# Where channel attention's two norms stand: inside the stages around them instead of between them

## The reference, cut to what matters

```python
f = jax.nn.gelu(h @ W1[l] + b1[l], approximate=False)
h = layer_norm(h + f @ W2[l] + b2[l], ln2_s[l], ln2_b[l])        # l = 3: the last of four layers
...
h = h + _L0_attn_ref(_layernorm(h, axis=-1), W_qkv, W_proj, b_proj, temp)   # channel attention
h = h + _L0_ffn_ref(_layernorm(h, axis=-1), Wg, bg, W1, b1, W2, b2)         # gates, then experts
...
def _L0_attn_ref(x, W_qkv, W_proj, b_proj, temp):      # per batch row, 8 heads of 24 channels
    q = q / jnp.linalg.norm(q, axis=1, keepdims=True)
    k = k / jnp.linalg.norm(k, axis=1, keepdims=True)
    attn = jax.nn.softmax(jnp.einsum('bnhd,bnhe->bhde', q, k) * temp, axis=-1)
    y = jnp.einsum('bhde,bnhe->bnhd', attn, v).reshape(b, n, c)
    return y @ W_proj + b_proj
```

## Time and profile before

| what | us |
|---|---|
| median of 3 runs (lowest, highest) | 1809.26 (1800.43, 1809.82) |
| the profiled execution, device time | 1813.13 |
| its span | 1811.3 |
| PE, DVE, ACT, POOL busy in the span | 1465.9, 1236.5, 980.9, 815.2 |
| PE's last product of layer 3 ends | 1003.27 |
| first products of channel attention start | 1037.99 |
| last product of channel attention ends | 1138.40 |
| the gates are complete (DVE reads them) | 1171.25 |

### The profile page before, as it was taken

The page is one execution under the profiler, slowest core; times in us unless marked ns, Lnnn a source line. Parts: engine busy times, 40 slices in busy tenths (PEclk is TensorE's granted clock), DMA queues, the critical chain, the costliest instruction groups (busy, mean ns, idle before and its releaser), DMA issues.

```text
span 1811.3 us, 39511 instructions
## 1 busy us (share of the span) xinstructions
PE 1465.9 (81%) x13098; PEld 1256.1 (69%) x13098; DVE 1236.5 (68%) x3514; ACT 980.9 (54%) x2393; POOL 815.2 (45%) x1175
## 2 busy tenths in 40 slices
PE   2789799997998888988989488669478887499991
PEld 2578677786777777877778377269457666499991
DVE  6878876889768896688976722434478886444444
ACT  1578635887348883378843133245258872055550
POOL 7786235773347733378523200145365511145540
PEclk9799999999999999999999678579789996599996
DMA  4644004470026530174800000167345501267765
GB/s 114 163 89 106 1 1 123 105 145 11 1 62 146 115 60 1 25 182 89 226 2 1 14 1 1 47 207 244 115 97 119 102 2 47 102 198 243 239 199 182
DMA packets 144278, 177.87 MB, mean 98 GB/s; under 512 B 22096, under 2 KB 106128, under 8 KB 143952
## 3 DMA queue, kind: packets, MB, share of 16 engines
q1 hardware_dynamic: 136784, 158.18, 34.0%
q0 software_dynamic: 7296, 17.18, 2.8%
HBM read 132.96 MB, written 42.34 MB: 97 GB/s over the span
## 4 chain that ended last, share of the span: by engine, by line
PE 53%; DVE 23%; issue 8%; POOL 8%; DMA 4%; ACT 3%; SPq 1%; POOLq 0%; DVEq 0%; ACTq 0%
PE bank L1498 7%; PE bank L663 7%; DVE ptl L821 4%; PE bank L575 4%; DVE neg_max L814 3%; PE bank L427 3%; PE bank L445 2%; PE bank L1484 2%; PE bank L447 2%; PE bank L446 2%; PE bank L449 2%; PE bank L448 2%; DVE xx L788 2%; PE bank L540 2%; DVE row_b L821 1%
## 5 line engine op out<-in xcount | busy, mean ns | idle before, releaser
L703 ACT ACTIVATE prob<-bank,neg_max 128x192 f32<-128x192 f32 (+1 forms) x960 | 412.6, 440 | 117.5 <-DVE neg_max L814 108.9
L814 DVE TENSOR_REDUCE neg_max<-bank 128x2 f32<-128x384 f32 (+1 forms) x480 | 272.2, 569 | 70.6 <-PE bank L540 69.9
L575 PE MATMUL bank<-ident,prob 128*128 128x128 f32 x1536 | 272.1, 290 | 48.3 <-DVE ptl L821 36.1
L716 ACT ACTIVATE pth<-bank 128x384 f16<-128x384 f32 (+1 forms) x480 | 245.9, 512 | 5.7 <-PE bank L575 5.6
L821 DVE TENSOR_TENSOR ptl<-bank,pth 128x384 f16<-128x384 f32 (+1 forms) x352 | 204.5, 581 | 10.5 <-ACT pth L716 10.0
L575 PEld LDWEIGHTS bank<-ident,prob 128*128 128x128 f32 x1536 | 161.7, 142 | 65.0 <-DVE ptl L821 47.6
L670 ACT ACTIVATE xx<-bank 128x256 fp32r<-128x256 f32 x256 | 96.3, 390 | 176.1 <-PE bank L427 172.6
L540 PE MATMUL bank<-kx,qx 96*128 96x192 bf16 (+1 forms) x960 | 166.8, 255 | 1.4 <-DVE xx L788 1.1
L754 ACT ACTIVATE fbuf<-bank,b 128x512 f32<-128x512 f32 x96 | 66.0, 687 | 165.0 <-PE bank L449 165.0
L596 PE MATMUL bank<-v,pth 128*128 128x33 bf16 x1152 | 137.8, 179 | 21.5 <-DVE ptl L821 18.5
L663 PE MATMUL bank<-w,fbuf 128*128 128x192 f32 x768 | 140.7, 326 | 1.9 <-DVE h L914 1.9
(11 more groups left out here) (304 smaller groups left out, 4644.7 us busy)
## 6 DMA issues: line engine op xcount, KB each, us to landing
xn<-in_e_seg SPq DMA_DIRECT2D x34, 768.0 KB, 6.7
w<-in_e_w SPq DMA_DIRECT2D x23, 576.0 KB, 4.3
qk_rows<-fbuf SPq DMA_DIRECT2D x128, 96.0 KB, 2.3
qx<-qk_rows SPq DMA_DIRECT2D x35, 288.0 KB, 4.1
kx<-qk_rows SPq DMA_DIRECT2D x35, 288.0 KB, 5.9
qk_rows<-w SPq DMA_DIRECT2D x80, 96.0 KB, 2.3
qx<-qk_rows SPq DMA_DIRECT2D x35, 192.0 KB, 4.7
kx<-qk_rows SPq DMA_DIRECT2D x35, 192.0 KB, 5.4
```

Source lines behind the costliest of these rows:

```text
L575: last = nc.tensor.transpose(bank[BT[p % 2]][:, c * P:c * P + P], probs_at(p, banded, c * P, P), ident[:, :])
L703: nc.scalar.activation(probs_at(p, banded, qt * n, n), scores_at(p, n)[:, qt, :], ACT.Exp, bias=neg_max[:, b % 2, hd, qt:qt + 1], scale=1. ...
L716: nc.scalar.activation(high_at(p, banded), bank[BT[p % 2]][:, 0:n], ACT.Copy).then_inc(hi_ready.sem, 1)
L814: nc.vector.tensor_reduce(neg_max[:, b % 2, hd, :], scores_at(p, D if banded else S), AX.X, ALU.max, negate=True).then_inc(max_ready.sem, 1)
```

## The change

The norm in front of channel attention and its turns leave their own stage:

- `dve_tail`, `pool_tail`, layer 3 alone: the statistics and the root of this norm for a group follow the affine of that group's second norm; its `dve_normalise` follows one iteration later, ahead of the next group's affine. The order of results on the shared counter is the new table `NORMED_LAST`.
- `under` hangs the turn of group 0 into step 16 of the feed-forward and that of group 1 into step 24. DVE splits group 0 (`channels(0)`) at the head of its iteration 3 and group 1 at the head of iteration 4.
- The turns of groups 2 and 3 and the `dve_normalise` of group 3 stand in the first two iterations of the batch loop. Batch b now waits for its own tiles (`xx_ready`) and for the release of the last feed-forward banks (`y_read`).
- The norm behind channel attention goes into the batch loop: DVE does the statistics of a group after iterations 2, 4, 6 and 8, its `dve_normalise` after iterations 3, 5 and 7 and after the loop. POOL does the roots between its powers.
- SP issues the ten loads of constants for this stage after layer 3's attention instead of after layer 3. Two memsets on POOL move ahead of the tail. PE waits for the lists and the last residual sum in front of the first gate product instead of implicitly through the norm.

No instruction of computation is added or removed.

```diff
@@ under
+            if channels:
+                steps[2 * FC + 4] = lambda: channels(0)
+                steps[NG * FC] = lambda: channels(1)
@@ dve_tail
+            def channels(g):
+                for t in range(GT * g, GT * g + GT):
+                    dve_split(dve, L, t, t)
...
+                if g >= NG - 1 and not opening:
+                    channels(g - NG + 1)
                 if g:
                     dve_residual(dve, ch, it, 1, g - 1)
                     dve_stats(dve, ch, it, 1, g - 1, y_read)
+                if g >= 2 and not opening:
+                    dve_normalise(dve, ch, it, norm_at(it, 0, g - 2), g - 2)
...
                 if g + 2 < NG:
                     out(g + 2)
+                if g and not opening:
+                    dve.wait_ge(h_ready.sem, h_ready.at(it, normed(2, GT * g - 1)))
+                    dve_stats(dve, ch, it, 0, g - 1, None)
@@ pool_tail
+                if g and not opening:
+                    scale(0, g - 1)
@@ sync
-            sp.wait_ge(h_ready.sem, h_ready.at(L, 0))
+            sp.wait_ge(sums_ready.sem, sums_ready.at(L - 1, NT))
@@ gpsimd
-            for g in range(NG):
-                pool_rstd(pool, ch, L, g + 1, g, 1e-5)
             for b in range(B):
...
+                if b and b % 2 == 0:
+                    pool_rstd(pool, ch, L, NG + b // 2, b // 2 - 1, 1e-5)
@@ scalar
-            for t in range(NT):
-                act_split(act, L, t, t)
             for b in range(B + 1):
                 if b < B:
                     act_xc_front(act, b)
+                if b < 2:
+                    xc_split(2 + b)
@@ vector
-            dve_norm_in(dve, ch, L, 0, 0)
...
                 if b:
                     dve_xc_out(dve, b - 1)
-            dve.wait_ge(xc_o_ready.sem, xc_o_ready.at(0, NT))
-            dve_norm_in(dve, ch, L, 1, None)
+                if b == 0:
+                    for t in range(2 * GT, 3 * GT):
+                        dve_split(dve, L, t, t)
+                    dve_normalise(dve, ch, L - 1, norm_at(L - 1, 0, 3), 3)
+                    for t in range(3 * GT, 4 * GT):
+                        dve_split(dve, L, t, t)
+                if b >= 3 and b % 2:
+                    dve_normalise(dve, ch, L, NG + (b - 3) // 2 + 1, (b - 3) // 2)
+                if b and b % 2 == 0:
+                    dve.wait_ge(xc_o_ready.sem, xc_o_ready.at(0, 2 * b))
+                    dve_stats(dve, ch, L, 0, b // 2 - 1, None)
+            dve_normalise(dve, ch, L, 2 * NG, NG - 1)
@@ tensor
-            for t in range(NT):
-                pe_transpose(pe, L, t, t, xn, xn_ready, 0, t + 1)
             pe.wait_ge(wa_ready.sem, wa_ready.at(L, 1))
-            pe.wait_ge(xx_ready.sem, xx_ready.at(L, NT))
...
+            pe.wait_ge(y_read.sem, y_read.at(L - 1, NT))
             for b in range(B + 1):
                 if b < B:
+                    pe.wait_ge(xx_ready.sem, xx_ready.at(L, 2 * b + 2))
                     pe_xc_front(pe, b)
                     pe_xc_gram(pe, b)
+                if b == 1:
+                    xc_turn(3)
+                    pe.wait_ge(xx_ready.sem, xx_ready.at(L, NT))
...
+                if b == 0:
+                    xc_turn(2)
```

More of the change, by code:

```diff
@@ L366, in normed, with norm_at @@
             return GT * NORMED.index((k, t // GT)) + t % GT + 1
+        def norm_at(it, k, g):
+            return (NORMED_LAST if it == LAYERS - 1 else NORMED).index((k, g)) + 1
         def turn_at(t, inside):
@@ L512, in early_steps, with under @@
             return list(zip(at, OPENING))
-        def under(turn, out=None, first=None):
+        def under(turn, out=None, first=None, channels=None):
             steps = {}
@@ L939, in dve_normalise @@
                 last.then_inc(xn_ready.sem, 1)
-        def dve_norm_in(dve, ch, it, half, turn):
-            for g in range(NG + 2):
-                if g < NG:
-                    dve_stats(dve, ch, it, half, g, None)
-                if 1 <= g <= NG:
-                    dve_normalise(dve, ch, it, half * NG + g, g - 1)
-                if turn is not None and g >= 2:
-                    for t in range(GT * (g - 2), GT * (g - 1)):
-                        dve_split(dve, it, turn * NT + t, t)
         def dve_affine(dve, ch, it, n, g, w):
@@ L970, in dve_tail @@
         def dve_tail(dve, ch, it, opening):
-            first = lambda g: NORMED.index((1, g)) + 1
-            second = lambda g: NORMED.index((2, g)) + 1
+            first = lambda g: norm_at(it, 1, g)
+            second = lambda g: norm_at(it, 2, g)
+            def channels(g):
+                for t in range(GT * g, GT * g + GT):
+                    dve_split(dve, L, t, t)
             def out(g):
@@ L1819, in pool_layer @@
                     pool_scale(pool, it, f)
+                if not opening:
+                    nc.gpsimd.memset(xc_nh[:, :], -0.5)
+                    nc.gpsimd.memset(xc_one[:, :], 1.0).then_inc(zeroed.sem, 1)
+                    pool.wait_ge(zeroed.sem, 2)
                 pool_tail(pool, ch, it, opening)
@@ L1841, in _ @@
                 .then_inc(lists_ok.sem, 1)
-            for g in range(NG):
-                pool_rstd(pool, ch, L, NG + g + 1, g, 1e-5)
+            pool_rstd(pool, ch, L, 2 * NG, NG - 1, 1e-5)
             pool_seq(pool, 0)
@@ L1888, in first_split, with xc_split @@
                 return lambda t, inside=False: act_split(act, it, t, t, inside)
+            def xc_split(g):
+                for t in range(GT * g, GT * g + GT):
+                    act_split(act, L, t, t)
             def act_layer(it, opening):
@@ L2105, in first_open, with xc_turn @@
                 pe_open(pe, it, kind, i, wa, first_turn(it), lambda n: (it, n))
+            def xc_turn(g):
+                for t in range(GT * g, GT * g + GT):
+                    pe_transpose(pe, L, t, t, xn, xn_ready, 0, t + 1)
             def pe_layer(it, opening):
@@ L2112, in pe_layer @@
                                 lambda g: pe_out_group(pe, it, wb, g),
-                                (lambda kind, i: first_open(it + 1, kind, i)) if opening else None))
+                                (lambda kind, i: first_open(it + 1, kind, i)) if opening else None,
+                                None if opening else xc_turn))
             for kind, i in OPENING:
@@ L2149, in _ @@
                                                    third[0:4, t * P:t * P + P], ident[0:4, 0:4])
+                if g == 1:
+                    pe.wait_ge(lists_in.sem, 32)
+                    pe.wait_ge(xc_o_ready.sem, xc_o_ready.at(0, 2 * B))
                 if 1 <= g <= NG:
```

8 lines of the change are left out of this document (3 added, 5 removed).

## The result

The changed kernel takes 1790.62 us (median of 7 runs, 1785.42 to 1793.25), the kernel before 1808.28 (7 runs, 1800.43 to 1814.6): a ratio of 0.9896, 95% interval 0.9869 to 0.9924, which is 14 to 24 us. The forecast was 1795.9 us, that is 13.4 us less, with a range of 1787.0 to 1806.0. The profiled executions stand further apart than the medians: 1785.42 against 1813.13, 27.7 us.

The account below looks back on a forecast made before the run. TensorE was taken to bound the tail, with two norm stretches where it waits for VectorE. Gains of 9.8 and 5.4 less 1.75 made 13.4 us off 1809.26, so 1795.9 us, range 1787 to 1806.

Parts of the forecast that it names:

- Part 1: Tail, step 16: TensorE stalls some 6 us for VectorE's splits of group 0's turn and loses clock; shift 9.6 us.
- the rival on hidden turns: Tail: turns cost less because the affine is faster without POOL beside it; about 1794, counted in the forecast's share.
- the fall of the clock: Tail, behind the stall at step 16: TensorE drops to half rate for a while, taken as 2.0 us.
- Part 2: Tail, step 24: TensorE waits for VectorE's late splits at group 1's turn; shift grows to 11.8 us.
- Part 3: Tail's end to the loop's first reciprocal, at 1045.0 instead of 1054.81: 9.8 us remain as the first norm's gain.
- Part 4: Batch loop: new norm work lies under VectorE's waits except ahead of the last probabilities, 1.75 us more.
- the loop has no cover: Batch loop: all of VectorE's new work counts, 10.4 us instead of 1.75, giving 1804.5; chance 10%.
- Part 5: Loop's end to gates: groups 0 and 1 are transposed at once, first gate product earlier, a gain of 5.4 us.
- What follows depends on the gates and moves with them: Behind the first gate product: the rest only shifts earlier with it, with no further gain counted.
- the gates run at full clock: Gates: if the missing 4.50 us gap kept the clock low, half of 25.29 us is saved too, 1783; chance 5%.
- the lost idle time ahead of the last reciprocal: Sign at the loop's end: VectorE's 0.36 us idle ahead of the last batch's probabilities is gone.
- near 28: Sign: first front to first reciprocal takes near 28 us; otherwise, or without a tail stall, the first three parts are wrong.

Follow-up runs that it names:

- a1: The changed kernel unaltered, run again: 1787.96 us against 1813.52 for the kernel before on this chip, ratio 0.986.
- a4: The changed kernel with group 0's turn in the tail called in step 18 instead of 16: 1781.87 us, ratio 0.9828.
- a3: The changed kernel with the second norm put back behind the batch loop, so only the first norm is moved: 1795.51 us, ratio 0.9898.
- b2: The changed kernel with TensorE waiting for group 3's normalisation before group 1's gate transposes: 1799.81 us, ratio 0.9933.
- c3: a3 unaltered, run again for a second profiled execution: 1794.86 us, ratio 0.9929.
- d1: b2 with the second norm's group 2 normalised behind the last batch's probabilities instead of ahead of them: 1790.35 us, ratio 0.9867.
- b4: a4 with the second norm's group 2 normalised behind the last batch's probabilities instead of ahead of them: 1781.79 us, ratio 0.9838.
- b1: The kernel before unaltered, run again for a second profiled execution: 1812.8 us, ratio 1.0.

## Why the forecast came out, and what was wrong in it

The time lies in the range and on the forecast side, 5.3 us below the number. The sum behind it was wrong by 11.4 us for the profiled executions (13.4 against 24.84), and by 4.3 for the medians of the first comparison. That the number came so near is in part luck: in a1's comparison the gain is 25.6 us, and 25.6 less than the 1809.26 from which the forecast counts is 1783.7, outside its range. By steps:

- **Part 1, group 0's turn.** The mechanism was right: VectorE's order, the wait of 5.11 us ("some 6 us"), half clock behind it. The term was too large, 9.6 us against 7.65 (group 2's residual sum stands 22.12 us behind group 1's, 14.47 before). Of the 1.95 us, 1.0 is the affine, which took 3.53 us and not 4.53 (the rival on hidden turns had named this), and 0.8 the fall of the clock. It cost about 1.2 us here and not 2.0: the tail is 5.41 us longer than a4's, of which 4.18 are the longer wait. But this price is one of several. With a wait of 5.11 or 5.09 us each time, the same reckoning gives 1.8 us for a1 and 2.5 to 2.6 for a3, b2, c3 and d1, so the forecast's 2.0 lies amid them.
- **Part 2, group 1's turn.** The shift grew by 2.24 us, 2.2 was forecast, and for a wrong reason. The forecast had TensorE wait until 1012.35 for late splits; VectorE was in fact ready at 1007.6 (for the reasons of Part 1, and with the affine 1 us shorter once more), before TensorE came at 1007.69. What costs is the turn itself. The sum had no price for a turn whose splits are ready; it only reckoned when VectorE would let TensorE go on. a4 shows it: with no stall at all, each turn costs 2.2 us.
- **Part 3, the first batch.** From the last product to the first reciprocal 28.37 us, against 29.95: the affine again (-1.0), POOL's queue 3.17 instead of 2.75 (+0.4), front and gram of batch 1 with its waits (-0.3), group 3's turn at full clock (-0.5), and 0.2 in small steps. With the tail's 1.9 it makes the gain of this norm 13.28 us (a1: 12.15) instead of 9.8.
- **Part 4, the loop.** +2.35 us against +1.75, and the reading was right: only the work ahead of the last probabilities has no cover (b4: 1.63 us), the rest 0.03. Of what remains, 0.45 also stands in a3 (76.80 against 76.35), which has no new work of the second norm there, and 0.24 between the changed kernel and a4 (78.46), whose loops hold the same work. The rival "the loop has no cover", which takes 10.4 us, is refuted.
- **Part 5, the gates.** The wait went as worked out, 5.80 us against 5.4. The failed step is "What follows depends on the gates and moves with them": it did not move, it shrank by 8.10 us. The rival "the gates run at full clock" is what the trace shows from the second half of the first gate product on, with 8.10 us where it had 12.6. The argument against it, that 25.29 of 28 us were busy at half clock and so idle time could not be the reason, was a fair reading of one execution; b2 against d1, and before against a3, point to a variable that it does not show, the place of the stretch in the clock's rhythm.

Of the signs named in the forecast, the stall, the lost idle time ahead of the last reciprocal and the gap of 4.46 us in front of the first gate product came as described. From the first front to the first reciprocal it took 26.75 us, a little below "near 28", for the reasons of Part 3, and the loop grew by less than the 3 us that would have spoken against Part 4.

The Trainium skill ("TensorE: Matmul & The Clock Gate", Part 1: The HAM clock gate) has it that the clock follows how busy the engine has been recently, and that the point at which it comes back depends on where the work falls. The second agrees with b2 and d1. The first does not explain the gates of the kernel before, if it is read by the profile's busy time: TensorE was busy 25.60 of 32.85 us, with no return in the 22.59 us from the first gate product on. Whether these transposes and narrow products (4 columns of weights) count as busy for the clock, no run here tested.

Open is why the medians show 17.7 us in the first comparison and 25.6 in a1, where the marks show 24.8 and 23.7. The runs of before spread over 22 us, their mean granted clock from 0.895 for the longest to 0.910 for the shortest, while its two profiled executions agree within 0.02 us in the sum of the marks. Part of the scatter lies outside the marks, where the profiled executions differ by up to 11.5 us ahead of the first and 10.4 behind the last. Whether the shorter runs of before have the clock back in the gates, as a3 does, no profile shows.

## To carry to other kernels

Work moved under a bound engine costs what it takes on that engine, stall or not; count the transposes as well as the wait for their splits. Look where the engine that feeds it has its last spare microsecond, and put the step one or two places later if it is late: here one number (step 18 for 16) was worth more than all other repairs. A gap of 4 us on TensorE can cost three times its length (3.95 us cost 11.9 in b2) or no more than itself (3.96 us cost 4.0 in d1, whose gates took 22.95 us against 18.95 in the changed kernel); when a gap between two stretches is closed, price the second stretch at both clocks, and treat the half clock after a gap as something that a shift of 2 us can make or undo.

## What the runs showed of the hardware

- **The clock's rhythm is inherited.** The distances between the reciprocals were 12.10, 10.88, 12.47, 9.28, 12.12, 10.92, 8.58 us before and 12.11, 10.89, 12.45, 9.28, 12.13, 10.93, 8.58 in b1, though everything stood 5.4 us later. Batches of one kernel do the same work and differ by up to 3.2 us, by how much of each ran at full clock: in before the batch of 9.28 us had a granted clock of 1.00, those of 10.88 and 10.92 us 0.84, those of 12.10 to 12.47 us 0.72 or 0.73. It is not wholly fixed by the program: the changed kernel and a1 (tail 36.71 and 37.31 us) begin with 12.9, 10.9, 12.3, and b2, which has the same instructions up to the gates (tail 38.07), with 12.4, 12.3, 9.3. Where the clock falls in the tail's stall may thus bear on the pattern of the 80 us behind it; no run tested that alone, and it is not the stall itself, since a4, which has none, begins with 12.4, 12.3, 9.3 too.
- **VectorE and POOL hold each other up in the affine, now the one, now the other.** Before, three of the four second halves took 0.68 us and POOL's row sums of that time 0.63 each (the last, with no affine beside it, 0.59). In the changed kernel all halves took 0.34 us and the four sums 3.58, 0.89 each:

```profile
982.44 3.58 POOL L1026 TENSOR_TENSOR hb<-h,row_bo 128x192 f32<-128x192 f32 x4 [2.25 <-DVE h L963]
```

  The Trainium skill ("SBUF — State Buffer", Who interferes with whom) calls the port pair that the two share an exclusive lock, held by whoever starts first for a whole instruction while the other blocks. The rows agree that either engine can be held up by the other; they do not show that one is blocked for the whole of the other's instruction, and no run here was made to test it. What set the alignment was not tried.
